# One stage of a decoder: the running sums of a rotating-memory layer taken with 64x64 weighted triangles in four quarters of the TensorE array

## What is computed

```python
z = causal_conv(x @ W_mem)                 # 32*8 values and 32 scores per token
p_w = exp(clip(scale * score, -20, 20) + log_w)          # [b, l, K]
phi = k_val[..., None] * theta                           # [b, l, K, H, M]
cs = cumsum([p_w, p_w * cos(phi), p_w * sin(phi)], axis=l)
den, num_re, num_im = cs
state_re, state_im = num_re / max(den, 1e-4), num_im / max(den, 1e-4)
out_re = sum_m(state_re * q_re + state_im * q_im)
out_im = sum_m(state_im * q_re - state_re * q_im)
y = out_re @ W_re + out_im @ W_im                        # per memory, 48 wide
y = (y_val * silu(y_gate)) @ W_out                       # added to x
```

## Time and profile before

| | us |
|---|---|
| median of 3 runs | 1846.21 (1841.38 to 1853.18) |
| profiled execution, its time | 1839.15 |
| profiled execution, its span | 1837.0 |
| second half of the fourth stage, first matmul to last residual add | 1086.88 to 1423.96 |

### The profile page before, as it was taken

The page is one execution under the profiler, slowest core; times in us unless marked ns, Lnnn a source line. Parts: engine busy times, 40 slices in busy tenths (PEclk is TensorE's granted clock), DMA queues, the critical chain, the costliest instruction groups (busy, mean ns, idle before and its releaser), DMA issues. The chain is left out here.

```text
span 1837.0 us, 32979 instructions
## 1 busy us (share of the span) xinstructions
PE 1634.2 (89%) x12606; PEld 1263.3 (69%) x12606; DVE 1133.4 (62%) x1852; ACT 844.2 (46%) x1403; POOL 684.0 (37%) x508
## 2 busy tenths in 40 slices
PE   4999999999996885798999688999998698999997
PEld 3888888888884663676888443444444475888886
DVE  6667776776776886665522868998996565111111
ACT  3555455455553663555422335555552574222222
POOL 0021211212123650900432108999995340333332
PEclk9999999999998996999999789999999898999999
DMA  3011111111112003001020100000000910000001
GB/s 100 16 61 56 43 52 57 66 40 58 51 43 87 2 2 97 10 10 27 19 101 0 38 0 0 1 1 0 1 1 1 344 39 1 1 1 1 1 0 46
DMA packets 67247, 67.73 MB, mean 37 GB/s; under 512 B 24208, under 2 KB 60560, under 8 KB 66496
## 3 DMA queue, kind: packets, MB, share of 16 engines
q1 hardware_dynamic: 67136, 66.19, 11.1%
HBM read 45.86 MB, written 19.27 MB: 35 GB/s over the span
## 5 line engine op out<-in xcount | busy, mean ns | idle before, releaser
L546 POOL TENSOR_TENSOR s_w_parts<-s_w_raw,s_w_parts 128x768 fp32r<-128x768 f32 x16 | 29.6, 1853 | 429.4 <-ACT s_w_parts L498 429.4
L1347 DVE TENSOR_TENSOR s6f_hid<-s6f_act_sb,s6f_u_ps 128x512 f32<-128x512 f32 x64 | 44.1, 688 | 218.4 <-PE s6f_u_ps L1298 218.4
L1370 POOL TENSOR_TENSOR s6f_hid_parts<-s6f_hid,s6f_hid_parts 128x512 fp32r<-128x512 f32 x64 | 82.2, 1284 | 225.4 <-ACT s6f_hid_parts L1336 225.4
L2012 POOL TENSOR_TENSOR s4b_pcs<-s4b_cs,s_p_rows 128x1024 f32<-128x1024 f32 x64 | 120.6, 1907 | 92.8 <-ACT s4b_cs L2058 89.4
L2023 POOL TENSOR_TENSOR s4b_with_re<-s4b_with_re,s4b_with_im 128x1024 f32<-128x1024 f32 x64 | 150.5, 2376 | 2.6 <-DVE s4b_with_im L1977 2.6
L2102 PE MATMUL s4b_c_ps<-s4b_pcs,const 128*128 128x512 f32 x256 | 121.6, 598 | 0.0
L422 PE MATMUL s_v_ps<-s_wv_parts,s_xnT 128*128 128x256 f32 x768 | 104.5, 286 | 11.8 <-ACT s_v L527 6.3
L481 PE MATMUL s_o_ps<-s_w_parts,s_zT 128*128 128x256 f32 x768 | 109.4, 292 | 4.1 <-DVE x_rows L585 4.1
L422 PEld LDWEIGHTS s_v_ps<-s_wv_parts,s_xnT 128*128 128x128 f32 x768 | 96.9, 191 | 17.4 <-ACT s_v L527 9.5
L1336 ACT ACTIVATE s6f_hid_parts<-s6f_hid 128x512 fp32r<-128x512 f32 x64 | 40.5, 632 | 144.3 <-PE s6f_o_ps L1318 140.8
L1318 PEld LDWEIGHTS s6f_o_ps<-s6w_parts,s6f_hid_parts 128*128 128x128 f32 x768 | 99.2, 188 | 6.8 <-issue 1.0
(11 more groups left out here) (314 smaller groups left out, 4017.2 us busy)
## 6 DMA issues: line engine op xcount, KB each, us to landing
stored_weights<-s1q_halves SPq DMA_DIRECT2D x16, 768.0 KB, 3.5
s6w_parts<-stored_weights SPq DMA_DIRECT2D x32, 384.0 KB, 7.9
s1q_packed<-in_codes SPq DMA_DIRECT2D x8, 384.0 KB, 4.5
s1q_scale<-in_scale_rows SPq DMA_DIRECT2D x8, 384.0 KB, 5.1
early_values<-s_vbd SPq DMA_DIRECT2D x1, 2176.0 KB, 11.9
s_vbd<-early_values SPq DMA_DIRECT2D x1, 2176.0 KB, 12.6
x_rows<-in_x SPq DMA_DIRECT2D x1, 2048.0 KB, 8.3
s_w_raw<-in_L_attn_W_Q SPq DMA_DIRECT2D x16, 128.0 KB, 2.2
```

What stands on the lines that cost most here:

```text
L1347: nc.vector.tensor_tensor(hid[:, f % 2, :], act_sb[:, f % 2, :], u_ps[:, f % 2, :], ALU.mult) \
L1370: nc.gpsimd.tensor_tensor(hid_parts[:, f % 2, 1, :], hid[:, f % 2, :], hid_parts[:, f % 2, 0, :], ALU.subtract).then_inc(low_done, 1)
L2012: last = nc.gpsimd.tensor_tensor(pcs[:, half, n_, :].rearrange("p (k c) -> p k c", k=HK), cs[:, half, n_, :].rearrange("p (k c) -> p k c", ...
```

## The change

The sums over tokens are taken per memory and per sequence. POOL multiplies a 64x64 triangle by the memory's p_w (a factor of the partition, so of the summed token), for 16 memories of a unit in one instruction, `tri_p`. This weighted triangle is the stationary operand; the unweighted cosines and sines of the memory, 128 columns side by side, are the moving one. Sequence b of the tile is in partitions 64b to 64b+63. For the lower eight memories of a unit (a = 0) the sums go to the sequence's own partitions, for the upper eight (a = 1) to those of the other sequence, so that all four 64x64 quarters of the array are used in turn. A call of `running_sums(n_)` is 16 matmuls; n_ now chooses four memories of each eight instead of cosine or sine. The queries, `den` and the turning of the results follow the exchange: the queries of the upper groups go through a second buffer and two DMAs a group, the denominators are taken with a second, exchanged triangle, and turn_outs is four fp32 matmuls, with the identity and with an exchanging matrix, in place of two transposes. The tables come with one more load. POOL's weight has lag 1 and doesn't wait for the sines; all parts behind it have one lag less (the products 2, the last part 8).

```diff
+def orders():
+
+    p = np.arange(P)
+    other = (p + S) % P
+    tri_seq = (p % S)[:, None] <= np.arange(S)[None, :]
+    tri_swapped = (p[:, None] <= other[None, :]) & (p[:, None] // S == other[None, :] // S)
+    return np.concatenate([tri_seq, tri_swapped, p[:, None] == other[None, :]], 1).astype(np.float32)
...
-        q_rows = oroom.sb("q_rows", [P, NT, QW])
+        q_rows = oroom.sb("q_rows", [P, 2, NT, 2, QW // 4])
...
+        LOADS2 = 16 * 6
+        order = oroom.sb("order", [P, S + 2 * P])
+        tri_seq, tri_swapped, swap = order[:, 0:S], order[:, S:S + P], order[:, S + P:]
...
+                sp.dma_start(order[:, :], ins["orders"]).then_inc(w2_in, 16)
...
+                for g in range(GROUPS):
+                    sp.wait_ge(q_out, TG * (g + 1))
+                    for b in range(2):
+                        src, dst = slice(b * S, (b + 1) * S), slice((1 - b) * S, (2 - b) * S)
+                        sp.dma_start(q_rows[dst, 1, g * TG:(g + 1) * TG, :, :], q_odd[src, g % 2, :, :, :]) \
+                            .then_inc(q_moved[g % 2], 16)
+                for moved in q_moved:
+                    sp.wait_ge(moved, 64)
...
-                                 start=True, stop=True).then_inc(d_full, 1)
+                pe.wait_ge(w2_in, LOADS2)
+                for a, tri in enumerate((core.c("tri"), tri_swapped)):
+                    last = nc.tensor.matmul(d_ps[:, a * 256:(a + 1) * 256], tri,
+                                            p_rows[:, :, :].rearrange("p t (h a k) -> p (t h) a k", h=2, a=2)[:, :, a, :],
+                                            start=True, stop=True)
+                last.then_inc(d_full, 1)
...
+                for a in range(2):
+                    nc.vector.tensor_scalar(den[:, :, :].rearrange("p t (h a k) -> p (t h) a k", h=2, a=2)[:, :, a, :],
+                                            d_ps[:, a * 256:(a + 1) * 256].rearrange("p (t k) -> p t k", k=8), 1e-4, None,
+                                            ALU.max)
...
                 for g in range(GROUPS):
+                    if g >= 2:
+                        act.wait_ge(q_moved[g % 2], 32)
                     for i in range(g * TG, (g + 1) * TG):
                         act.wait_ge(q_full, i + 1)
-                        nc.scalar.activation(q_rows[:, i, :], q_ps[:, i % 2, :], ACT.Copy).then_inc(q_out, 1)
+                        by_group = q_ps[:, i % 2, :].rearrange("p (h a c) -> p a h c", h=2, a=2)
+                        nc.scalar.activation(q_rows[:, 0, i, :, :], by_group[:, 0, :, :], ACT.Copy)
+                        nc.scalar.activation(q_odd[:, g % 2, i % TG, :, :], by_group[:, 1, :, :], ACT.Copy) \
+                            .then_inc(q_out, 1)
...
-            cs = room.sb("cs", [P, 2, 2, N])
-            pcs = room.sb("pcs", [P, 2, 2, N])
-            with_re = room.sb("with_re", [P, 2, 2, N])
-            with_im = room.sb("with_im", [P, 2, 2, N])
-            red = room.sb("red", [P, 2, 2, HK * H])
+            cs = room.sb("cs", [P, 2, HK, 2, H * M])
+            tri_p = room.sb("tri_p", [P, 2, HK, S])
+            with_re = room.sb("with_re", [P, 2, HK, 2, H * M])
+            with_im = room.sb("with_im", [P, 2, HK, 2, H * M])
+            red = room.sb("red", [P, 2, HK * 2 * H])
             outs = room.sb("outs", [P, 2, 2, HK * H])
...
-                v = q_rows[:, bass.ds(i, 1), half * QW // 2:(half + 1) * QW // 2]
-                v = v.rearrange("p t (g c two) -> p (t g) c two", g=2, two=2)[:, :, :, part]
+                v = q_rows[:, :, bass.ds(i, 1), half, :]
+                v = v.rearrange("p a t (c two) -> p (a t) c two", two=2)[:, :, :, part]
                 return v.unsqueeze(2).to_broadcast([P, 2, 8, H * M])
...
+                        for part, dst in ((0, with_re), (1, with_im)):
                             last = nc.vector.tensor_tensor(
-                                dst[:, half, at, :].rearrange("p (g k c) -> p g k c", g=2, k=8), src,
-                                q_view(i, half, part), ALU.mult)
+                                dst[:, half, :, :, :].rearrange("p (a n j) s c -> p a n (j s) c", a=2, n=2)[:, :, n_, :, :],
+                                src, q_view(i, half, part), ALU.mult)
                         last.then_inc(prod_done, 1)
                     return part
 
                 def reduce(u, i, half):
                     dve.wait_ge(sum_done, 2 * (u + 1))
                     wait(dve, outs_done, u - 1)
-                    nc.vector.tensor_reduce(red[:, half, :, :],
...
-                run_steps(dve, UNITS, [(multiply, 7), (add, 9), (reduce, 5), (fraction(0), 0), (products(0), 3),
-                                       (fraction(1), 0), (products(1), 3)])
+                run_steps(dve, UNITS, [(multiply, 6), (add, 8), (reduce, 4), (fraction(0), 0), (products(0), 2),
+                                       (fraction(1), 0), (products(1), 2)])
...
                 def weight(u, i, half):
-                    pool.wait_ge(cs_done, 2 * (u + 1))
                     wait(pool, c_full, 2 * (u - 1))
-                    for n_ in range(2):
-                        last = nc.gpsimd.tensor_tensor(
-                            pcs[:, half, n_, :].rearrange("p (k c) -> p k c", k=HK),
-                            cs[:, half, n_, :].rearrange("p (k c) -> p k c", k=HK),
-                            p_rows[:, bass.ds(i, 1), half * HK:(half + 1) * HK].rearrange("p t k -> p (t k)")
-                            .unsqueeze(2).to_broadcast([P, HK, H * M]), ALU.mult)
-                    last.then_inc(pcs_done, 1)
+                    nc.gpsimd.tensor_tensor(
+                        tri_p[:, half, :, :], tri_seq.unsqueeze(1).to_broadcast([P, HK, S]),
+                        p_rows[:, bass.ds(i, 1), half * HK:(half + 1) * HK].rearrange("p t k -> p (t k)")
+                        .unsqueeze(2).to_broadcast([P, HK, S]), ALU.mult).then_inc(weighted, 1)
...
                     for n_, op in ((0, ALU.add), (1, ALU.subtract)):
...
+                        nc.gpsimd.tensor_tensor(with_re[:, half, :, n_, :], with_re[:, half, :, n_, :],
+                                                with_im[:, half, :, 1 - n_, :], op).then_inc(sum_done, 1)
 
                 def scale(u, i, half):
...
+
+                run_steps(pool, UNITS, [(scale, 5), (weight, 1), (combine, 3)])
...
-                    wait(act, pcs_done, u - 1)
-                    nc.scalar.activation(cs[:, half, 1, :], frac[:, half, :], ACT.Sin, scale=-TWO_PI) \
+                    wait(act, c_full, 2 * (u - 1))
+                    nc.scalar.activation(cs[:, half, :, 1, :], frac[:, half, :].rearrange("p (k c) -> p k c", k=HK),
+                                         ACT.Sin, scale=-TWO_PI) \
                         .then_inc(cs_done, 1)
                     wait(act, cs_done, 2 * u)
                     nc.scalar.activation(afrac[:, :], frac[:, half, :], ACT.Abs).then_inc(abs_done, 1)
 
                 def cosines(u, i, half):
                     act.wait_ge(abs_done, u + 1)
-                    nc.scalar.activation(cs[:, half, 0, :], afrac[:, :], ACT.Sin, scale=-TWO_PI,
+                    nc.scalar.activation(cs[:, half, :, 0, :], afrac[:, :].rearrange("p (k c) -> p k c", k=HK),
+                                         ACT.Sin, scale=-TWO_PI,
                                          bias=core.c("half_pi")).then_inc(cs_done, 1)
...
-                run_steps(act, UNITS, [(gates, 7), (rounding(0), 0), (sines, 1), (yT_copy, 7), (outT_copy, 6),
+                run_steps(act, UNITS, [(gates, 6), (rounding(0), 0), (sines, 1), (yT_copy, 6), (outT_copy, 5),
                                        (rounding(1), 0), (cosines, 1)], head=UNITS + 7)
...
-                        pe.wait_ge(pcs_done, u + 1)
+                        pe.wait_ge(cs_done, 2 * (u + 1))
+                        pe.wait_ge(weighted, u + 1)
                         wait(pe, prod_done, 2 * u - 1 + n_)
-                        for b in range(N // 512):
-                            last = nc.tensor.matmul(c_ps[:, n_, b * 512:(b + 1) * 512], core.c("tri"),
-                                                    pcs[:, half, n_, b * 512:(b + 1) * 512], start=True, stop=True)
+                        for j in range(4):
+                            for a in range(2):
+                                for b in range(2):
+                                    rows, to = slice(b * S, (b + 1) * S), (a + b) % 2
+                                    k = a * 8 + n_ * 4 + j
+                                    last = nc.tensor.matmul(
+                                        c_ps[to * S:(to + 1) * S, n_, a, j * P:(j + 1) * P], tri_p[rows, half, k, :],
+                                        cs[rows, half, k, :, :].rearrange("p s c -> p (s c)"), start=True, stop=True)
                         last.then_inc(c_full, 1)
                     return part
...
-                    for n_ in range(2):
```

(49 more changed lines are left out.)

8 lines of the change are left out of this document (3 added, 5 removed).

## The result

| | before | changed |
|---|---|---|
| median of runs taken side by side | 1842.9 us (7 runs, 1839.85 to 1853.18) | 1830.12 us (7 runs, 1824.81 to 1836.85) |
| ratio, 95% interval | 1 | 0.9913 (0.9890 to 0.9935) |
| profiled execution, span | 1839.15, 1837.0 us | 1829.93, 1828.1 us |
| mean granted clock | 0.960 | 0.953 |

The changed kernel is 0.9% faster: 12.8 us by the medians, 16 us by the ratio. 1833 us were forecast. One slow execution of one experiment (e7, 2164.31 us, at a mean granted clock of 0.739) is left out of all numbers.

The account below looks back on a forecast made before the run. DVE was taken to set the main loop's period, with a 1.58 us wait for PE's output matmuls before each add. Terms: -8.4 - 4.7 + 0.3 = -12.8 us, a median of about 1833 us; range 1816 to 1856.

Parts of the forecast that it names:

- Running sums 1.11 us a call: Fourth stage, PE: a call falls from 1.81 to 1.11 us; bounds 1.0 and 3.7 us.
- Period 18.40, wait 0.88, 12 x 0.70 = -8.4: Fourth stage's main loop: period from 19.09 to 18.40 us, DVE's wait before the add from 1.58 to 0.88, 12 times.
- Filling -4.7: Fourth stage's second half: one step less lag brings the first reduce 4.7 us earlier; bounds 0 and -7.4.
- the chain: PE, ACT and DVE followed through the pipeline's filling: fourth products end, first reduce starts, at 1118.1 instead of 1122.84.
- GpSimd's relief worth nothing by itself: POOL's unit falls from 9.19 to 7.3 us; since POOL did not set the period, zero gain.
- turn_outs costs nothing under PE's waits: Four matmuls add 0.45 us a unit on PE, covered by its waits of 0.89 and 0.31 us; uncovered, 14 us.
- rival (d): Longer PE idle before even fractions makes the granted clock fall once in each of 14 periods: +11, 1857 us; chance 0.08.
- First half +0.3: Fourth stage's first half: DVE's clamp split in two and PE's matmul cut in two cost +0.3 us.
- Rival (a): PE's path falls under DVE's own, the wait goes entirely: -18.1, with -7 from filling, -25, 1821 us; chance 0.18.
- (b): Quarters sharing a PSUM bank wait for each other: 16 turns, 1.98 us a call, about +2, 1848 us; chance 0.14.
- (c): Quarters run one after the other: 3.7 us a call, PE the bound, +100 us, 1946 us; chance 0.05.
- The signs named: Fourth stage: add to add 18.4 us, wait 0.9 us, POOL near 79%, first reduce about 4.7 us earlier.

Follow-up runs that it names:

- e7: The kernel before with VectorE's residual add moved behind the reduce of the same step: 1835.11 us, ratio 0.9966.
- e5: The changed kernel without the exchange in the running sums, so only two quarters of the array are used: 1846.77 us, ratio 1.0032.
- e2: The changed kernel with a second GpSimd instruction of the weighting's size in each unit, into a tile nobody reads: 1833.48 us, ratio 0.995.
- e6: The changed kernel with turn_outs as two transposes again, sequences not exchanged back: 1839.75 us, ratio 0.9981.
- e1: The changed kernel with VectorE's residual add moved behind the reduce of the same step: 1817.83 us, ratio 0.985.
- e9: The changed kernel with turn_outs as two transposes, sequences not exchanged back, and the off-path running_sums(0) call done twice: 1826.05 us, ratio 0.9901.

## Why the prediction was right, and where it was not

The sum was -12.8 us and the medians differ by 12.8, but that is partly luck: the second half alone gives 16.8 and 17.8.

- *Running sums 1.11 us a call*: 1.03, near the forecast's lower bound of 1.0. It was worked out from the fifth stage's scores, and their 32 records do start in four groups of eight: at 1464.55, 1464.71, 1464.82 and 1464.93, within 0.05 us in a group, the first two groups 0.16 us apart and the others 0.109. That four quarters would make eight groups was an estimate; the changed kernel's call shows them. The 0.05 us ahead of it for the switch of tile shape were 0.10: phases to sums is 1.06 us where it was 0.96. Together 1.13 us. PE's path 7.31: 7.34.
- *Period 18.40, wait 0.88, 12 x 0.70 = -8.4*: the period is 18.25 and the wait 1.07. The path through PE gave 0.67 us, and **DVE's part of the period, which I had kept at 11.09 us (19.09 less 8.01 is 11.08), is 10.91**. One of its products came late in the kernel before and no longer does, which fits sums that are ready earlier. From the second fraction of a step to its products it was 0.76 us and is 0.60 (DVE, second profile of the kernel before, then the changed kernel):

```profile
1253.16 0.68 DVE L1962 SCALAR_TENSOR_TENSOR s4b_frac<-s4b_whole,s4b_turns_ps 128x512 f32<-128x512 f32 x1
1253.92 1.22 DVE L1977 TENSOR_TENSOR s4b_with_re<-s4b_c_ps,s_q_rows 128x1024 f32<-128x1024 f32 x1
```

```profile
1251.51 0.68 DVE L1995 SCALAR_TENSOR_TENSOR s4b_frac<-s4b_whole,s4b_turns_ps 128x512 f32<-128x512 f32 x1
1252.11 1.22 DVE L2010 TENSOR_TENSOR s4b_with_re<-s4b_c_ps,s_q_rows 128x1024 f32<-128x1024 f32 x1
```

  So the period lost 0.85 us in place of 0.70: over the stretch from first to last reduce 11.0 us without a fall of the clock (second profile), 10.15 with one. This term was too small by 1.8 to 2.6 us.
- *Filling -4.7*: -7.1 and -7.3. No run shows the chain that the 4.7 was worked out from: it took the granted clock of 0.50 over from the kernel before, where it stood at 1100.5 to 1107.3 us (1103.0 to 1109.8 in its second profile). Around that place, second profiles of the kernel before and of the changed one:

```profile
1092.00:1108.00 16.00, 11.93 (x21) 3.92 (x20) 6.55 (x6) 9.03 (x11) 3.76 (x2) 0.82 0.00 0
```

```profile
1092.00:1108.00 16.00, 12.02 (x85) 5.24 (x84) 8.86 (x9) 10.58 (x12) 0.09 (x1) 0.98 0.00 0
```

  In the changed kernel the half clock at that place is absent: it ended 6 and 5 us after the first phases, and the mean is 1.00 from there until after the first reduce. The first sums start 15.6 us after the first phases (1107.49 in the first profile), as in the chain (1100.57 + 1.91, after phases at 1086.88). But the chain let them take 2.2 us at the half clock, and they took 1.10 at 1.00. e5, whose calls are as long as the old ones, fills in 31.3 us, which is the forecast's -4.7, also at a granted clock of 1.00 (1094 to 1130 us); so the faster calls carry some 2.5 us more. How the 4.7 is shared between the lag and the clock was not separated. In the experiments on the changed kernel the filling took 28.7 to 31.3 us.
- *GpSimd's relief worth nothing by itself*: right (e2), and e7 points to when it counts.
- *turn_outs costs nothing under PE's waits*: the 0.45 us (0.37 by the idle times of e6) are covered, as far as that goes; they show only in the tail (+0.5 us). **The step that failed is the price of taking cover away from a waiting engine: zero.** e6 shows it: without them the idle time is 1.94 instead of 1.57 us, the clock falls in 7 of 11 periods of its profile, and 9.6 us are lost by the medians. I had the mechanism as rival (d), with 0.08, but weighed it only for idle times of 1.8 us and did not see that the four matmuls were what kept the kernel out of it.
- *First half +0.3*: not to be seen; 57.5 against 57.0 us in the second pair.
- *Rival (a)*: its size, -25 us, is what e1 reaches (1818), by moving the add and not by a shorter path. *Rivals (b) and (c)*: refuted by the 1.03 us of a call, in eight groups of four records, where (b) had 1.98 us in sixteen turns and (c) 3.7 us. No wait shows where two row halves write different partitions of the same bank.
- The signs named: 18.25 for 18.4, 1.07 for 0.9, POOL 78.1% for 79%, the first reduce 7.1 us earlier for 4.7.

## What to carry to other kernels

Follow the wait that ends last to the one call that stands in it: of the two kinds of call made faster in each step here, one carried the steady gain, and moving the waiting instruction behind one that needs nothing from it gave as much again (e1, 12 us). When work is taken from an engine that waits, look at its idle time as well as at its path: here the time was 10 us longer with 0.4 us more of it on TensorE (e6: 1.94 us in place of 1.57, 1839.75 us in place of 1830.12). And profile both kernels twice before a few microseconds in a stretch that the change hardly touches are explained.

## What the runs showed of the hardware

- Less work, more time (e6), and falls of the granted clock to 0.50, 3.4 us each, counted beside PE's idle time ahead of the even phases: with 1.94 us in 7 of 11 periods (e6, one profile; the seven are 19.76 to 19.88 us long, the other four 18.25); with 1.57 us in one of 22 (changed kernel, two profiles) and one of 11 (e2), each 19.82 us long; with 1.07 us in none of 11 (e9). These are counts in five profiled executions; what brings a fall about they do not show.
- Four quarters of 64x64 ran at once: the call's 32 records of 128 columns start in eight groups of four, and the next instruction starts 1.03 us after the first of them (changed kernel, 1250.44 to 1251.47). With two quarters they start in sixteen pairs, and the call took 1.89 us (e5). Row halves that write the same bank, in different partitions, did not wait for each other (changed kernel, the same call).
- A GpSimd tensor_tensor over 128x1024 elements took 1.904 us as a multiply of two operands that are both broadcast views (changed kernel), as of one full and one broadcast (kernel before, 1.904); as an add or a subtract of two full ones it took 2.369 (changed kernel).
